# Last stage of a one-core sandwich kernel: the recurrence's output rows are normalised by ScalarE instead of VectorE, and two VectorE steps move in its order

## The reference, cut to what matters

```
x = x + norm(window_attention(norm(x)))
x = x + norm(top-2 of 8 experts + shared expert (norm(x)))
x = x + norm(linear_attention(norm(x)))     # q, k = silu, rotated; causal energy; running state; gate; own norm
x = x + norm(recurrence(norm(x)))           # two steps over the two halves of the rows
recurrence: c0 -> (gates f, i, candidate) -> c1 -> c2 ; h = tanh(x @ wo.T + c2 @ uo.T + bo)
```

## Time and profile before

| | |
|---|---|
| times of the kernel before, us | 1414.31, 1415.17, 1417.53 (median 1415.17) |
| profiled execution, us | 1415.55, its span 1413.5 |
| mean granted TensorE clock of the span | 0.996 |
| busy share of the span | PE 97%, PEld 82%, DVE 67%, ACT 49%, POOL 42% |
| last stage | from about 905 us to the end |

### The profile page before, as it was taken

How to read it: one execution, slowest core, us unless ns; L and a number is a source line. 1 busy time by engine, 2 the same in 40 slices (tenths; PEclk the granted TensorE clock), 3 DMA queues, 4 the chain that set the end, 5 groups by cost and what they waited for, 6 DMA issues and landing times. The chain is left out here.

```text
span 1413.5 us, 37117 instructions
## 1 busy us (share of the span) xinstructions
PE 1373.1 (97%) x13346; PEld 1155.1 (82%) x13346; DVE 943.2 (67%) x2208; ACT 695.3 (49%) x1620; POOL 595.6 (42%) x1121
## 2 busy tenths in 40 slices
PE   7999999999999999999999999999999999999995
PEld 6888888788988888888888899777877778787785
DVE  5888888475365555555555532477888888888774
ACT  4666666313444444444444333344555565565553
POOL 3656665233212121212121111646577776776433
PEclk9999999999999999999999999999999999999998
DMA  5433434352111111111111132521211111121000
GB/s 163 126 114 111 132 114 124 119 183 69 42 46 42 42 39 50 39 42 50 43 42 50 38 101 72 173 78 47 61 47 54 61 58 58 46 58 47 10 10 30
DMA packets 88723, 100.02 MB, mean 71 GB/s; under 512 B 12320, under 2 KB 75808, under 8 KB 88544
## 3 DMA queue, kind: packets, MB, share of 16 engines
q1 hardware_dynamic: 80928, 79.04, 18.0%
q0 software_dynamic: 6240, 17.05, 4.2%
q10 hardware_dynamic: 1376, 1.57, 0.3%
HBM read 63.80 MB, written 33.82 MB: 69 GB/s over the span
## 5 line engine op out<-in xcount | busy, mean ns | idle before, releaser
L1022 POOL COPY slot_idx<-source 128x1 int32<-128x1 int32 x58 | 21.3, 367 | 391.2 <-PE wa_Z L1191 376.2
L1058 PE MATMUL wa_P<-ex_xT,lane_w 128*128 128x128 f32 x1440 | 170.7, 275 | 0.0
L1200 PE MATMUL wa_Y<-w,ex_gT 128*128 x720 | 166.2, 380 | 1.6 <-DVE ex_gT L1272 0.9
L1058 PEld LDWEIGHTS wa_P<-ex_xT,lane_w 128*128 128x128 f32 x1440 | 165.7, 192 | 0.2 <-issue 0.2
L1200 PEld LDWEIGHTS wa_Y<-w,ex_gT 128*128 128x128 f32 x720 | 132.1, 190 | 18.9 <-issue 3.2
L1058 PEld LDWEIGHTS wa_qv<-ex_xT,lane_w 128*128 128x128 f32 x720 | 90.6, 191 | 17.9 <-issue 17.4
L1058 PE MATMUL wa_qv<-ex_xT,lane_w 128*128 128x128 f32 x720 | 103.6, 280 | 0.0
L2108 POOL DMA_INDIRECT la_a<-yg,place x64 | 66.8, 1043 | 66.3 <-PE la_E L1702 35.9
L1270 DVE TENSOR_TENSOR ex_gT<-ex_gT,wa_xk 128x256 f32<-128x256 f32 x60 | 25.1, 418 | 103.7 <-ACT ex_gT L1232 103.7
L1230 ACT ACTIVATE ex_gT<-wa_qv 128x256 f32<-128x256 f32 x60 | 23.1, 384 | 138.1 <-PE wa_qv L1058 136.1
L1054 ACT COPY lane_w<-w 128x1408 f32 x60 | 82.0, 1366 | 6.4 <-issue 1.2
(11 more groups left out here) (327 smaller groups left out, 3451.9 us busy)
## 6 DMA issues: line engine op xcount, KB each, us to landing
yg<-ex_yo SPq DMA_DIRECT2D x60, 128.0 KB, 1.7
w<-in_w SPq DMA_DIRECT2D x16, 384.0 KB
w<-in_w SPq DMA_DIRECT2D x16, 352.0 KB, 3.1
w<-in_w SPq DMA_DIRECT2D x16, 320.0 KB, 4.0
wa_xa<-in_x SPq DMA_DIRECT2D x32, 128.0 KB, 2.1
x<-wa_xo SPq DMA_DIRECT2D x32, 128.0 KB, 1.7
xn<-wa_xn SPq DMA_DIRECT2D x32, 128.0 KB, 2.1
xn1T<-wa_x1T SPq DMA_DIRECT2D x32, 128.0 KB, 2.3
```

Of the source, the lines that this page charges most:

```text
L1058: o = e.matmul(out, lane_w[:, i % 2, k, at:at + P], B[i % 2]["xT"][:, k, :], start=(k == 0), stop=(k == KC - 1))
L1200: o = e.matmul(yb[:, 0:C], gT[:, k, :], w2[:, bass.ds(KF * y + k, 1), :], start=(k == 0), stop=(k == KF - 1))
```

## The change

ScalarE gets a function `output_norm`, called between the gate and `oT`, for all pairs but the last. It needs scale and shift, so POOL computes a third column `hnm` (two instructions for a pair) behind the power. VectorE loses L1857 (it stays with the last pair's own form). `kr` is made behind the gates' products rather than right after `qr`, by the helper `rotated`. The statistics "0" of ym move from before y to behind y's own statistics.

```diff
-                ("hst", [P, 2, 6]), ("hmv", [P, 2, 2]), ("hve", [P, 2]), ("hrs", [P, 2]))})
+                ("hst", [P, 2, 6]), ("hmv", [P, 2, 2]), ("hve", [P, 2]), ("hrs", [P, 2]), ("hnm", [P, 2]))})
...
+        def rotated(e, i, x, n):
+
+            d, u = B[i % 2], i // 2
+            cos_sin = CS[u % 2][:].rearrange("p x (h d) -> p h x d", h=HEADS)
+            e.wait_ge(S["qks"], i + 1)
+            e.wait_ge(S[f"cs{u % 2}"], 16 * (u // 2 + 1))
+            if i >= 2:
+                e.wait_ge(S["tq" if n == "qr" else "U"], i - 1)
+            if i >= 2 and n == "kr":
+                e.wait_ge(S["tk"], i - 1)
+            e.tensor_tensor(d[n][:].rearrange("p (h x d) -> p h x d", h=HEADS, x=2),
+                            bc(d["qks"][:, x].rearrange("p (h d) -> p h d", h=HEADS), 2, 2), cos_sin,
+                            ALU.mult).then_inc(S[n], 1)
...
                 for i in tile(s, 4, NT):
-                    d, u = B[i % 2], i // 2
...
-                    for x, n in enumerate(("qr", "kr")):
...
+                    rotated(e, i, 0, "qr")
                 for t in tile(s, 10, NT):
...
+                for i in tile(s, 4, NT):
+                    rotated(e, i, 1, "kr")
                 for u in pair(s, 13):
-                    p = H[u % 2]
-                    e.wait_ge(S["rsh"], 2 * u + 2)
-                    for q in range(2):
-                        if u < PAIRS - 1:
-                            o = e.tensor_scalar(p["h"][:, q], p["h"][:, q], p["hmv"][:, q, 0:1], p["hrs"][:, q:q + 1],
-                                                ALU.subtract, ALU.mult)
-                        else:
+                    if u == PAIRS - 1:
+                        p = H[u % 2]
+                        e.wait_ge(S["rsh"], 4 * u + 2)
+                        for q in range(2):
                             e.wait_ge(S["hc"], 1)
                             e.scalar_tensor_tensor(...)
-                    if u < PAIRS - 1:
-                        o.then_inc(S["aph"], 1)
...
-                    e.wait_ge(S["y1"], i + 1)
-                    norm_stats(e, S, "0", i, d["ln0"], d["ym"][:], 3)
...
                     norm_stats(e, S, "1", i, d["ln1"], d["y"][:], 2)
+                for i in tile(s, 1, NT):
+                    e.wait_ge(S["y1"], i + 1)
+                    norm_stats(e, S, "0", i, B[i % 2]["ln0"], B[i % 2]["ym"][:], 3)
...
+        def output_norm(e, u):
+            p = H[u % 2]
+            e.wait_ge(S["rsh"], 4 * u + 4)
+            for q in range(2):
+                o = e.activation(p["h"][:, q], p["h"][:, q], ACT.Identity, scale=p["hrs"][:, q:q + 1],
+                                 bias=p["hnm"][:, q:q + 1])
+            o.then_inc(S["aph"], 1)
...
                     e.activation(d["gt"][:], d["gt"][:], ACT.Copy, scale=0.5, bias=0.5).then_inc(S["gt"], 1)
+                for u in pair(s, 13):
+                    if u < PAIRS - 1:
+                        output_norm(e, u)
                 for i in tile(s, 5, NT):
...
-                    e.wait_ge(S["rsh"], 2 * u + 1)
+                    e.wait_ge(S["rsh"], 4 * u + 1)
...
                     e.tensor_tensor(p["hrs"][:], p["hve"][:], half.broadcast_to([P, 2]), ALU.pow).then_inc(S["rsh"], 1)
+                    if u < PAIRS - 1:
+                        e.wait_ge(S["rsh"], 4 * u + 2)
+                        for q in range(2):
+                            e.tensor_scalar(p["hnm"][:, q:q + 1], p["hmv"][:, q, 0:1], p["hrs"][:, q:q + 1], -1.0, ALU.mult,
+                                            ALU.mult).then_inc(S["rsh"], 1)
```

More of the change, by code:

```diff
@@ L1817, in vector @@
                 for i in tile(s, 4, NT):
-                    d, u = B[i % 2], i // 2
-                    cos_sin = CS[u % 2][:].rearrange("p x (h d) -> p h x d", h=HEADS)
-                    e.wait_ge(S["qks"], i + 1)
-                    e.wait_ge(S[f"cs{u % 2}"], 16 * (u // 2 + 1))
-                    for x, n in enumerate(("qr", "kr")):
[L1823 to L1829, removed]
+                    rotated(e, i, 0, "qr")
                 for t in tile(s, 10, NT):
```

## The result

| | before | after |
|---|---|---|
| median of seven runs each, us | 1415.17 (1413.72 to 1417.66) | 1421.84 (1420.89 to 1424.84) |
| profiled execution, us | 1415.55 | 1421.96, its span 1420.2 |
| mean granted TensorE clock of the span | 0.996 | 0.994 |

A forecast was written before the change was run, and what follows sets the result against it. PE was taken to bound the steady part, with no slack for VectorE in odd steps. 5.0 - 1.05 + 0.2 + 2.5 = +6.65 us gave 1421.8 us against the median, range 1415 to 1427.

The forecast's parts named there:

- Steady collision: Odd steps s = 13 to 29: POOL's later `result` holds VectorE's yn and yb; nine pairs of 0.55, +5.0 us.
- Other odd steps: s = 7, 9, 11, 31, 33: VectorE's tail gains 0.13 each, s = 31 another 0.4; −1.05 us.
- Even steps: Statistics "0" behind y add 0.57 before the mask, of 0.58 to give; 0.02 over 12 pairs, +0.2 us.
- kr's move: `kr` behind the gates' products: PE takes its transposes several us later; cost 0, −0.1 to +0.1 a pair.
- ScalarE's norms: Two rows' norms per pair, 1.2 us together, fit ScalarE's 1.38 of idle time in steady steps; cost 0.
- Drain: From s = 37: w(29) waits behind ScalarE's norm, +2.05, and s = 39 adds 0.45; +2.5 us, between +1.5 and +3.3.
- No collision: POOL catches up and `result` still misses yn; 14 odd steps give 0.13, +0.5 in all, 1415.7 us; chance 0.18.
- Collisions in full: yn and yb each held a whole half of `result`, 1.3 net nine times; +13, or 1427 to 1428 us; chance 0.10.
- Faster: VectorE's relief ends PE's wait at L1664, 0.4 a pair, 14 times, −5.6; 1410 to 1412 us; chance 0.09.

The follow-up runs named there:

- all three corrections: The kernel after with `result` ahead of the gathers, ScalarE's norm last in its drain steps and statistics "0" ahead of y, against the kernel before: 1413.50 us (0.9983).

## Why the prediction was right

The time was forecast at 1421.8 us and came at 1421.84. That the two agree to 0.04 is luck: in the stretches that hold nearly all that the forecast priced (9–27, 27–31 and the rest) the profiles differ by 7.4, not by 6.65, and what it had not priced brought −0.7. Term by term:

- **Steady collision, +5.0 (nine pairs of 0.55).** Stretch 9–27, which holds these nine pairs and nothing else that was forecast but 0.2, grew by 4.8; the odd steps grew by 0.45 to 0.49 each, that of s = 27, with VectorE's 0.25 of idle time, by 0.84. The records of yn and yb grew by 0.28 and 0.35, together 0.63 (forecast 0.7). y gained 0.69 (0.70 at most) and the statistics cost 0.54 (0.57). `result` came 1.0 later behind z, not 1.2. That the collision is the cause is shown: with `result` moved ahead of the gathers it is gone, and 5.6 us with it.
- **Other odd steps −1.05.** At s = 31 the step went from 15.12 to 14.61: −0.51, forecast −0.53. The other four brought no 0.13. Of them PE had waited for the mask only at s = 9, not at 7, 11 and 33, and in all four nothing of VectorE's own stood between z and y before, so y had nothing to gain. At 11 and 33 the step kept its length (14.61, 14.36). At 7 and 9 the statistics had been free and now cost PE: it idles 0.39 for the mask at s = 7, where it did not before, and 1.39 for 0.91 at s = 9. This term was a misreading; these four are worth +1.0 and not −0.5, which the sum of the profile hides.
- **Even steps +0.2.** 0.02 a step. y follows z as before, and L1664 starts without a wait. The margin at the mask held. But the statistics alone cost 0.16 a step, by way of POOL and `qr`; in the change kr's move takes that away.
- **ScalarE's norms 0 in steady steps.** Held: `oT` starts 0.98 behind the norm's start (the norm's two records overlap it by a little), and 1.3 before z needs it.
- **kr's move 0, between −0.1 and +0.1 a pair.** Right for the kernel before (+0.1 a pair), wrong in the change: with POOL late by its columns it saves 5.9 to 6.1 us in nine pairs, 0.7 each. The forecast of the whole was not hurt, since its sum had no price for the even steps' collision (`qr` and `kr` held by x2 and xo) that the move avoids. It was right there for a reason that it had not seen. By its own rule (POOL later by 1.2 in an odd step) it should have asked what else of POOL moves, in even steps too.
- **Drain +2.5.** Measured +3.1. ScalarE's wait was where it was put: w(29) stands behind a norm that waits 2.48 and starts 2.74 later (forecast 2.76). PE's wait, 3.30, is ahead of L1620, which turns w, not ahead of L1514. L1514 starts 2.81 later, and the first products with the weights u* (L1511) 2.79, where the forecast had 2.05 left. The 0.7 that was to come back, with the idle time of 0.52 ahead of the next L1620, went to the stretch at 1.2 GHz, in which L1525's and L1514's eight products last 1.92 and 1.87, not 1.06 each as at 2.4 GHz back to back. L1525's part of that lay in PE's wait for the copy of wT. That s = 39 then adds 0.3 and not 0.45 makes up a little.

**The rivals.** "No collision" is refuted by yn and yb. "Collisions in full" asked for both held by 0.71; they were held by 0.28 and 0.35. "Faster" stood on y starting before z, or on statistics that cost nothing behind y; both failed (0.04 and 0.54). Its gain of 0.4 a pair was too large even where its condition is met: with all three corrections it is 0.26. PE's odd step, from L1669 to L1669, is then 0.35 shorter (14.36 against 14.71), but the even one 0.10 longer.

Not forecast: 0–1 became 1.3 shorter and 1–9 2.4 longer. The statistics behind y do both by themselves (9.75 and 117.60 with that part alone). Of the 1.3, 0.55 is of the run: 0–1 took 11.02 and 10.47 in the two profiles of before. Of the 2.4, 1.7 is a stretch at half clock (below) and 1.0 the statistics at s = 7 and 9; s = 10 gives back 0.56, as it does with kr's move alone.

## What to carry to other kernels

Work moved from a loaded engine to an idle one carries preparation with it; here two POOL instructions a pair, on 128 numbers each, cost 8 us by themselves, and VectorE's relief gave back 0.5. Where two engines just miss each other on long rows (0.04 us), price the delay of either one first, and in every step that the delayed engine passes through. Ahead of a point where the engine waits anyway (ym ahead of z) such a collision cost nothing here; moving `result` there, with the statistics ahead of y as before and the norm last in ScalarE's drain, turned the loss of 6.7 us into a gain of 2.4.

## What the runs showed of the hardware

- **Small columns are stretched when VectorE is busy with SBUF operands.** The pair of `hnm` took 0.50 in the drain (above), where VectorE stood idle, and 1.13 in the steady step, 1.26 with the columns and kr's move, 1.76 with the columns alone, where VectorE works on its products meanwhile. The forecast counted 0.65 to 0.7 by the earlier trace rows. The Trainium skill ("SBUF — State Buffer", section "Who interferes with whom") tells of VectorE and GpSimd holding each other off; the traces agree for yn (0.45 to 1.01) and `qr` (0.69 to 1.12), and show that 128x1 operations pay too.
- **Half-clock stretches.** A stretch of 3.4 us with the granted clock at 1.2 GHz made the products in it 1.7 us longer; in the drain about 0.7 of that came through, an estimate from L1511's start (2.79 later, 2.05 without it by the forecast's sum). The one in the drain is in all five profiles in which ScalarE's norm stands ahead of w(29) (after twice, three experiments), each behind an idle time of PE of 3.3 us, and in none of the other nine, where PE idled 1.1 at most for a w. Another, at 970 us, comes behind no such idle time. In these stretch tables, of the second profile of before and of the kernel after, PE was equally busy just ahead of it:

```profile
955.00:970.00 15.00, 14.50 (x180) 12.09 (x179) 11.14 (x29) 6.66 (x16) 9.95 (x22) 1.00 0.21 64
970.00:974.00 4.00, 4.00 (x32) 1.87 (x31) 1.89 (x3) 1.50 (x5) 1.25 (x2) 1.00 0.21 66
```

```profile
955.00:970.00 15.00, 14.50 (x180) 12.07 (x179) 10.55 (x29) 6.25 (x16) 9.87 (x20) 1.00 0.22 64
970.00:974.00 4.00, 4.00 (x7) 1.40 (x5) 1.29 (x2) 0.60 (x1) 1.54 (x3) 0.57 0.21 66
```

It is in eight of nine profiles of kernels that have the statistics or the norm moved, both of after among them, in one of the two of all three corrections, and in none of the five others. The norm has not begun there, so its cause stays open, and whether it belongs to the change. It makes 1.7 of the 2.4 in 1–9. A third, at 274 us, far ahead of the changed stage, is in the first profile of before and not in its second, whose stretch to tile 0 is 1.5 shorter. The first profile of after lacks it, so it may make most of the −1.8 to tile 0. But the second of after has it and still needs 903.17, so other things move that stretch as much.
- **What stays open.** The two profiles of all three corrections differ by 5.3 us at equal steady steps. 1.7 of it is the clock at 970 and 1.7 that at 274; the other 1.9, before the last stage, has no cause here. By this much one profile's total can miss, which is why the readings of parts go by stretches. Open too is VectorE's idle time of 0.25 at s = 27.
